# GpSimd waits for its own stores and ends with a small memset, in a one-core graph-transformer layer

## The reference

```python
x = x + gnn(layernorm(x), adj, ...)   # 4 heads of 32: masked softmax attention, @ Wo + residual, layernorm
x = x + ffn(layernorm(x), ...)
# ffn: gate scores for 8 experts, the 2 best per token; for those two
#      y = gelu(t @ W1[e] + b1[e]) @ W2[e] + b2[e], summed; all others are masked to zero
```

## Time and profile before

| | |
|---|---|
| median of three runs | 727.55 us |
| the profiled execution's own time | 729.22 us |
| its span, first to last instruction | 727.49 us |
| TensorE busy | 689.7 us (95%), 5510 matmuls |
| VectorE busy | 590.7 us (81%) |
| GpSimd busy | 564.9 us (78%), 155 of its instructions indirect DMAs |
| ScalarE busy | 538.6 us (74%) |
| mean granted TensorE clock | 0.992 |

### The profile page before, as it was taken

One profiled execution on the slowest core, in us unless ns is written; L12 is line 12 of the kernel. 1 busy time (PEld: TensorE's weight loads), 2 busy tenths in 40 slices (PEclk: granted clock), 3 DMA queues, 4 the chain that ended last, 5 costly groups with the idle time before them and its releaser, 6 DMA issues.

```text
span 727.5 us, 17325 instructions
## 1 busy us (share of the span) xinstructions
PE 689.7 (95%) x5510; PEld 364.0 (50%) x5510; DVE 590.7 (81%) x1270; ACT 538.6 (74%) x1225; POOL 564.9 (78%) x627
## 2 busy tenths in 40 slices
PE   8997999999999999999999999989888999999994
PEld 6421333333333333333333333323378899999994
DVE  4789989898999989999998999999897655555552
ACT  4776787888878788887888887666676566667662
POOL 7759696989889898988988889898776776545553
PEclk9999999999999999999999999999999999999997
DMA  7450010010100101111010010013241354333300
GB/s 259 157 167 30 1 30 15 17 45 30 45 34 27 45 15 45 45 31 45 16 45 23 27 43 15 30 54 108 62 130 55 97 157 125 97 96 102 105 26 2
DMA packets 47961, 45.45 MB, mean 62 GB/s; under 512 B 6981, under 2 KB 42576, under 8 KB 47872
## 3 DMA queue, kind: packets, MB, share of 16 engines
q1 hardware_dynamic: 41888, 31.60, 15.5%
q0 software_dynamic: 5984, 12.74, 5.0%
HBM read 27.73 MB, written 18.34 MB: 63 GB/s over the span
## 4 chain that ended last, share of the span: by engine, by line
PE 69%; DVE 15%; issue 6%; ACT 5%; DMA 1%; DVEq 1%; SPq 1%; POOLq 0%; POOL 0%; ACTq 0%
PE scores_ps L455 15%; PE ctx_ps L467 11%; DVE e L1029 10%; PE scores_ps L631 9%; PE z_ps L474 9%; PE ctx_ps L657 5%; PE z_ps L657 5%; ACT x_rows L784 3%; PE job_ps L503 2%; PE job_ps L530 2%; PE job_ps L494 2%; PE job_ps L566 2%; ACT e L779 1%; PE job_ps L515 1%; PE job_ps L565 1%
## 5 line engine op out<-in xcount | busy, mean ns | idle before, releaser
L779 ACT ACTIVATE e<-e 128x2048 f32<-128x2048 f32 x128 | 245.1, 1915 | 109.3 <-DVE e L1029 108.5
L1029 DVE SCALAR_TENSOR_TENSOR e<-scores_ps,bound_mem 128x2048 f32<-128x2048 f32 x128 | 293.2, 2290 | 40.0 <-PE scores_ps L455 34.6
L901 ACT ACTIVATE e<-scores_ps,bound_mem 128x128 f32<-128x128 f32 x364 | 104.4, 374 | 51.0 <-PE scores_ps L631 51.0
L1533 POOL DMA_INDIRECT out<-e,near x91 | 91.0, 1000 | 62.0 <-DVE e L1253 49.0
L474 PE MATMUL z_ps<-e,one_column 128*32 128x512 f32 x1024 | 133.3, 592 | 0.0
L1514 POOL TENSOR_TENSOR ctx_part<-ctx_part,z_inv 128x1024 f32<-128x1024 f32 x60 | 115.5, 1925 | 18.2 <-DVE z_inv L1045 18.1
L1526 POOL TENSOR_TENSOR ctx_sum<-ctx_sum,ctx_part 128x512 f32<-128x512 f32 x90 | 115.7, 1285 | 8.4 <-POOL ctx_sum L1526 0.9
L631 PE MATMUL scores_ps<-e,bound_mem 128*128 128x128 f32 x728 | 97.0, 276 | 4.0 <-ACT e L872 2.1
L1037 DVE STREAM_TRANSPOSE ctx_part<-ctx_ps 128x512 f32<-128x512 f32 x128 | 90.3, 705 | 1.6 <-PE ctx_ps L467 1.6
L631 PEld LDWEIGHTS scores_ps<-e,bound_mem 128*128 128x128 f32 x728 | 88.5, 192 | 5.6 <-ACT e L872 3.9
L1488 POOL DMA_INDIRECT sorted_rows<-x_rows,slot x64 | 63.5, 993 | 19.3 <-issue 16.1
(11 more groups left out here) (194 smaller groups left out, 1055.8 us busy)
## 6 DMA issues: line engine op xcount, KB each, us to landing
near<-sorted_rows SPq DMA_DIRECT2D x91, 130.0 KB, 2.2
near<-in_x SPq DMA_DIRECT2D x16, 256.0 KB, 2.8
bound_mem<-in_adjT SPq DMA_DIRECT2D x4, 1024.0 KB, 10.0
x_post<-in_x SPq DMA_DIRECT2D x16, 256.0 KB, 2.7
sorted_rows<-pad_row SPq DMA_DIRECT2D x1, 3640.0 KB, 15.3
out<-e,near POOLq DMA_INDIRECT x91, 2.3
sorted_rows<-x_rows,slot POOLq DMA_INDIRECT x64
bound_mem<-in_w SPq DMA_DIRECT2D x1, 1024.0 KB, 5.7
```

The lines of the kernel that those rows point to most:

```text
L779: nc.scalar.activation(every, every, ACT.Exp, scale=SCORE_SCALE).then_inc(exp_done, 1)
L901: nc.scalar.activation(e_flat[:, h_at:h_at + P], scores_ps[:, i % 2, k * P:(k + 1) * P], ACT.Gelu, bias=part_flat[:, bias_at:bias_at + 1]) ...
L1029: dve.scalar_tensor_tensor(out=e[:, s % E_RING], in0=scores_ps[:], scalar=-CLIP, in1=to, op0=ALU.max, op1=ALU.min).then_inc(clipped, 1)
L1533: nc.gpsimd.indirect_dma_start(out=out_rows, out_offset=bass.IndirectOffsetOnAxis(ap=near_u[:, id_at:id_at + 1], axis=0), in_=e_flat[:, at ...
```

## The change

After its last store GpSimd waits for every one of the 16 store semaphores at its full count, the same wait that SyncE has, and then sets the first column of `done_col` (28 x 1) to zero. Nothing reads the column after that. Nothing else is changed.

```diff
@@ -1612,6 +1612,9 @@
                 if k == 13:
                     scatter(15, (2, 3))
                     scatter(15, (0, 1))
+            for r in range(XT_RING):
+                pool.wait_ge(out_stored[r], 16 * len(range(r, FFN_TILES, XT_RING)))
+            nc.gpsimd.memset(done_col[:, 0:1], 0.0)
```

## The result

The changed kernel takes 729.35 us (median of 22 runs) against 727.51 us for the kernel before (22 runs): +1.84 us, ratio 1.0027, 95% interval 1.0019 to 1.0034, which is 1.4 to 2.5 us. The forecast was +1.85 us. Ratios in this document are estimated from all executions of both kernels and are not the quotient of the two medians.

A forecast was written before the change was run, and what follows sets the result against it. GpSimd's closing DRAIN was taken to bound the end: free at 721.18 us, plus 7.93 of work and 0.23 for release, gives a 729.34 us span against 727.49, +1.85; median 729.4 us, range 721.3 to 730.8 us.

The forecast's parts named there:

- The end of the kernel is the end of GpSimd's DRAIN: At the block's end, GpSimd's DRAIN lasts 9450 ns, to 727.26 us, and the span is over 0.23 us later.
- The DRAIN doesn't wait for data, it works: Behind the last store, the DRAIN's 7.93 us is work for the indirect DMAs issued, not waiting for data.
- C: Rival, 13%: at the end, the DRAIN's work could start only when the last store was in; +0.67 us, 728.2 us.
- The work starts when GpSimd is free: At the end, the DRAIN's 7.93 us of work starts when GpSimd is free, at 721.18 us, and ends at 729.11.
- B: Rival, 13%: the work began when the DRAIN was issued, so all 9.45 us follow the new issue; +3.12 us, 730.7 us.
- The delay of 1.85 us: Ahead of the DRAIN, waits and memset leave GpSimd free at 721.18 us instead of 719.33, 1.85 us later.
- 51 ns for each indirect DMA: In the last DRAIN, 7.93 us of work divided by 155 indirect DMAs; marked as a guess.
- The guess that the older DMAs are worked off while the last one is on its way: In the old DRAIN, work on the 154 older DMAs goes first, so the wait removes nothing of 1.18 us.
- A: Rival, 27%: the last DRAIN was long from meeting unfinished stores and becomes 0.05 us; 6.03 us less, 721.5 us.
- D: Rival, 10%: the last DRAIN ends a fixed time after the last store, so the change doesn't reach the end; 727.55 us.
- the receipts: After the last store, a DRAIN waiting for write receipts would be released near 720.4 us; claimed not what it waits for.

## Why the prediction was right

*The end of the kernel is the end of GpSimd's DRAIN.* Shown by the version without it: the span's end moved from 8.16 to 2.01 us behind the last store.

*The DRAIN doesn't wait for data, it works.* Shown by the four kernels with 155 DMAs: 7.917 to 7.925 us whether the last store had landed or not, and whether a DMA, a memset or a wait stood ahead of it. This step carried the sign of the forecast. What I had to go on was that no packet moved in the last 7 us. It holds because the DMAs are many: with 23 and fewer the DRAIN's end is counted from the landing, as C has it.

*The work starts when GpSimd is free.* Right to some nanoseconds (7.925 and 7.924 us), and the term in which B differed. The start that the row gives is that of the instruction's issue.

*The delay of 1.85 us.* It measured 1.82. Its terms are off in both directions. From the last store's end to the first passed wait 1.18 us were expected and measured. From there to the start of the last of the six instructions it is 5 x 0.087 = 0.43 us, where I had six at SyncE's pace, 0.37; the memset starts 0.11 us behind that start, where the store's row had given 0.21; the memset's 0.09 us holds. So the two errors, 0.06 us too little and 0.10 too much, nearly cancel, and that the medians differ by 1.84 us, 0.01 from the forecast, is luck within an interval of 1.4 to 2.5 us. The mechanism is not luck: the trace shows it piece by piece. The two traces don't agree ahead of 717 us, as I had asked: the last store ends 0.47 us earlier after the change, which is within the spread of single executions, and so the DRAIN starts at 720.58 us and not near 720.9.

*51 ns for each indirect DMA.* Wrong, as a size and as a count: it is 82 ns for each of 96. I had marked it as a guess that the sum doesn't need, and it didn't, because the change leaves the number of DMAs as it was. The guess that the older DMAs are worked off while the last one is on its way fits what the short DRAINs show, for a first half of the work.

*The rivals.* A had 27%, and was the only one that would have made the change worth while. The idea behind it, that waiting first spares the wait later, is shown to be false here. D falls with A: the end moved with GpSimd's last instruction. As for the receipts, they bind with few DMAs: with 4 to 23 of them the DRAIN ended 0.21 to 0.98 us behind the last landing, and with 155 the landing left no mark.

## What to carry to other kernels

When the last microseconds of a span show no engine and no DMA busy, look at the sequencers' rows of the block's end, and measure a long DRAIN from the end of the instruction ahead of it, not from its own start. A GpSimd that issues DMAs pays for them in its next DRAIN, so keep that off the path to the end: leave it out where another engine already waits for every store (the times here bear that out, and nothing more than the times), or do it once earlier, at a place where GpSimd has slack. A wait in front of it only moves it.

## What the runs showed of the hardware

A DRAIN on GpSimd cost 0.05 us and 82 ns for each DMA, indirect or plain and of 16 or 128 partitions, that GpSimd had issued since its last DRAIN. With 33 DMAs and more it made no difference whether the last had landed; with 4 to 23 the DRAIN ended 0.04 us and 41 ns for each DMA after the last landing. The ordinary GpSimd instructions of the earlier trace rows did not pay for it. Ahead of the 114th indirect DMA since the last DRAIN GpSimd paused for 1.50 us, and by the lengths 59 DMAs were struck off there, so that a DRAIN after 114 cost 4.58 us where one after 104 cost 8.58. Plain loads of 128 partitions paused ahead of the 114th and those of 16 ahead of the 129th, and all loads before the pause were struck off.
